# One transformer layer on one core: the routed experts on rows sorted by expert group, in place of every expert on every row

## The chip, the cores and the metric

One core of one Trainium2 chip runs the whole kernel. The metric is the device time in microseconds (us) of one execution, as the median of the runs shown. All arithmetic is in 32-bit floats.

## The reference

The input x has 2048 rows of 256. Layer norm gives xn. Two branches work on xn and are added to x:

- Attention with fast weights. q, k, v and small gates are projected from xn. In chunks of 128 rows, a recurrence takes each chunk's gradients of three fast weight matrices for each of 4 heads, adds momentum, runs five Newton-Schulz iterations on them, adds the result to the weights and scales these to their old row norms. The next chunk needs the new weights, so the 16 chunks are strictly in turn. Beside it stands a windowed softmax attention over 128 + 128 rows. The sum is multiplied by Wo.
- A mixture of experts, cut to what matters:

```
scores = sigmoid(x @ gate_w.T);  sb = scores + gate_bias      # 32 experts in 4 groups of 8
group_scores = sum of the two best sb of each group;  keep the 2 best groups
topi = the 8 best sb of the kept groups
cw = scores at topi / their sum * 2.5, else 0
x_lat = x @ fc1_w.T                                            # 256 -> 128
h = relu(x_lat @ w1[e])**2 * cw[:, e]                          # 128 -> 128, for each expert e
routed = (sum over e of h @ w2[e]) @ fc2_w.T                   # 128 -> 128 -> 256
shared = relu(x @ shared_up.T)**2 @ shared_down.T              # 256 -> 512 -> 256
```

A row has a weight other than 0 for 8 experts at most, and all of these lie in 2 of the 4 groups.

## The kernel before, in words

The kernel is written by hand for five instruction streams (SP for DMA, GpSimd as POOL, ScalarE as ACT, TensorE as PE, VectorE as DVE). Each is executed in its own order and waits on semaphores, named e_... . The order in each stream is the schedule. It is one function, `build` (L74), with an inner function for each piece of work.

There are 16 tiles of 128 rows. Step i (`body(i, last)` in each stream) does the recurrence of tile i and prepares tile m = i + 1. A step has these parts:

- k_side (PE L673, ACT L471, DVE L1067, POOL k_u L331): the products with the fast weights and the gradients' factors, then grads (PE L682), momentum (DVE L1100), the sums for the norm (PE L693, POOL ss_pow L335) and x_first (DVE L1118), which writes X.
- A loop over 20 stages, `for st in range(4 * NI)`, for the two head pairs g = 0 and 1. Four stages are one Newton-Schulz iteration: PE turns X (L697), ACT copies XT (L476), PE makes the Gram product (L703), DVE copies it to Am (L1129), PE squares it (L718), DVE makes Mp (L1134), PE multiplies (L718), DVE makes the new X (L1142). POOL makes aX = a * X at the iteration's start (ax, L339), which DVE's new X needs. After stage st each stream does what its table `fill` has for st: the projections, norms, attention and small gates of tile m or i. This is how all other work is spread through the loop.
- After the loop: update (DVE L1158), row_pow (POOL L345), renorm (DVE L1166, scaling in L1175), turn_w (PE L726) and w_T (ACT L480), which give the next step its weights.

The experts are 8 units (NU) of 4 experts (EU) for each tile. Every expert is computed for every row:

- h_up (PE L825): 4 products of the expert weights with xlT (fc1's result, L805) into the PSUM bank HB.
- h_relu (ACT L507), then h_sq (POOL L358): hr, then hq, 128x512 each.
- y_down (PE L833): 4 products of hq with the second weights into the bank YB.
- y_first (ACT L513) and y_acc (DVE L1321): acc += cw[e] * y, one instruction for each expert (L1328). y_sum (L1331) adds the four parts; turn_y (PE L840), y_T (ACT L537) and out_fc2 (PE L862) end the routed branch in the same bank as the output.

Units 0 and 1 of the next tile are done between the steps, the others at listed places of the step. The routing of tile m is 13 small DVE instructions (route, L1256, rows 128x32 and less), one of which is taken at each half stage after stage 10, and weights (L1316). Layer norm of tile m is ln_stats (L990), prep_rstd on POOL (L287), ln_norm (L998), a transpose on PE (L632) and a copy on ACT (L428). Matmuls issued through a helper are all recorded at L629, ACT's instructions at L426, POOL's powers at L285: go by tile names.

All weights are loaded once at the start (SP L243 to L250, ACT L416 to L423), the two expert tensors with 2 MB each. In a step SP (L261 to L268) loads the next x tile, stores the output tile and loads x again for the residual.

Of the kernel before, what the change touches and what calls it, by code (L numbers as in the profile page):

```python
# [29 lines left out]
F32 = mybir.dt.float32  # L30
AX_X = mybir.AxisListType.X

P = 128
# [13 lines left out]
NU = E // EU  # L47
# [25 lines left out]

def build(nc, x, wall_d, rows_d, wo, fast_d, affine_d, fc1T, fc2T, e1T, e2T, upT, downT, ident_d, fixed_d, out):  # L74
    T = x.shape[0]
    NT = T // P
    LAST = NT - 1
    with ExitStack() as ctx:
        def sb(name, shape):
            return ctx.enter_context(nc.sbuf_tensor(name, shape, F32))  # L80

# [9 lines left out]
        fc1_s = sb("fc1_s", [P, KT, P])  # L91
# [3 lines left out]
        e1_s = sb("e1_s", [P, E, P])  # L95
        e2_s = sb("e2_s", [P, E, P])
# [32 lines left out]
        xa = sb("xa", [P, D])  # L129
        xr = sb("xr", [P, D])  # L130
        ot = sb("ot", [P, D])
        st6 = sb("st6", [P, 6])
        mv = sb("mv", [P, 2])
        rstd = sb("rstd", [P, 2])
        xn = sb("xn", [P, D])
        xnT = sb("xnT", [P, KT, P])
# [6 lines left out]
        z = sb("z", [P, SMALL])  # L143
        sgs = sb("sgs", [P, SMALL - MOM])
# [29 lines left out]
        sbias = sb("sbias", [P, E])  # L174
        g8 = sb("g8", [P, NG, 8])
        gs = sb("gs", [P, 12])
        t8 = sb("t8", [P, 8])
        gm = sb("gm", [P, 12])
        pen = sb("pen", [P, NG])
        msk = sb("msk", [P, E])  # L180
        m8 = sb("m8", [P, 8])
        mr = sb("mr", [P, E])
        csel = sb("csel", [P, E])
        cs1 = sb("cs1", [P, 2])
        cw = sb("cw", [P, E])
        xlT = sb("xlT", [P, P])
        ur = sb("ur", [P, SC, P])
        us = sb("us", [P, SC, P])
        hr = [sb(f"hr{b}", [P, EU, P]) for b in range(2)]
        hq = [sb(f"hq{b}", [P, EU, P]) for b in range(2)]  # L190
        acc = sb("acc", [P, EU, P])
        ya = sb("ya", [P, 2, P])
        ys = sb("ys", [P, P])
        yT = sb("yT", [P, P])
# [11 lines left out]
        def per_group(name):  # L206
# [3 lines left out]
        e_const, e_later, e_up_w, e_down_w, e_ttw, e_init = (sem(n) for n in (  # L210
            "first_const_in", "later_const_in", "up_weights_in", "down_weights_in", "fast_weights_in", "init"))
        e_xa, e_xr, e_stored = sem("xa_in"), sem("xr_in"), sem("stored")
        e_stats, e_aggr, e_veps, e_rstd, e_xn = (sem(n) for n in ("stats", "aggr", "veps", "rstd", "xn_ready"))
# [10 lines left out]
        e_up, e_rn, e_rp, e_wn, e_bd, e_wt, e_WT = (per_group(n) for n in ("upd", "rn", "rp", "Wn", "W1BD", "wt", "WT"))  # L224
# [5 lines left out]
        e_rt, e_cw = sem("route_steps"), sem("cw_ready")  # L230
        e_lr_steps, e_nmx = sem("lr_sum_steps"), sem("max_ready")
        e_fx, e_xlT, e_upm, e_ur, e_us = (sem(n) for n in ("fc1", "xlT", "shared_up", "shared_relu", "shared_sq"))
        e_h, e_hr, e_hq, e_y, e_acc = (sem(n) for n in ("h", "h_relu", "h_sq", "y", "acc"))
        e_ya, e_ys, e_yt, e_yT, e_out, e_ot = (sem(n) for n in ("ya", "y_sum", "y_turned", "yT", "out_mm", "out_ready"))

        NCONST, NLATER, NUP, NDOWN = 2, 3, 3, 3
# [4 lines left out]
        @block.sync  # L241
        def _(sp):
            sp.dma_start(xa[:, :], x[0:P, :]).then_inc(e_xa, 16)  # L243
            sp.dma_start(ident[:, :], ident_d[:, :]).then_inc(e_ident, 16)
            for dst, src in ((wall[:, :, :], wall_d[:, :, :]),
                             (rows[:, :], rows_d.partition_broadcast(P))):
                sp.dma_start(dst, src).then_inc(e_const, 16)
            for dst, src in ((fixed[:, :, :], fixed_d[:, :, :]), (affine[:, :, :], affine_d[:, :, :]),
                             (wo_s[:, :, :], wo.rearrange("(k p) n -> p k n", p=P))):
                sp.dma_start(dst, src).then_inc(e_later, 16)  # L250

            sp.wait_ge(e_xn, 1)
            sp.dma_start(xa[:, :], x[P:2 * P, :]).then_inc(e_xa, 16)
            sp.dma_start(xr[:, :], x[0:P, :]).then_inc(e_xr, 16)

            def store(i, rows):

                sp.wait_ge(e_ot, i + 1)
                sp.dma_start(out[bass.ds(rows, P), :], ot[:, :]).then_inc(e_stored, 16)

            for i in range(NT - 2):  # L261
                here, after, later = i * P, (i + 1) * P, (i + 2) * P

                sp.wait_ge(e_xn, i + 2)
                sp.dma_start(xa[:, :], x[bass.ds(later, P), :]).then_inc(e_xa, 16)
                store(i, here)

                sp.dma_start(xr[:, :], x[bass.ds(after, P), :]).then_inc(e_xr, 16)  # L268
            store(NT - 2, (NT - 2) * P)
            sp.dma_start(xr[:, :], x[LAST * P:T, :]).then_inc(e_xr, 16)  # L270
            store(LAST, LAST * P)
            sp.wait_ge(e_stored, 16 * NT)


        @block.gpsimd
        def _(pool):

            win_scores = Expect(pool, e_as, "win_scores", first=2)
# [86 lines left out]
            def body(i, last):  # L365
                if last:
# [5 lines left out]
                    for u in range(4, NU):  # L372
                        h_sq(i, u)
# [1080 lines left out]
```

## Time and profile before

| what | value |
|---|---|
| median of 3 runs | 831.35 us (829.08 to 831.86) |
| the profiled execution's own time | 830.14 us |
| its span, first to last instruction | 828.1 us |
| PE busy | 780.7 us, 94% |
| DVE busy | 714.6 us, 86% |
| ACT busy | 354.0 us, 43% |
| POOL busy | 406.8 us, 49% |
| bytes moved by DMA | 15.09 MB, of it over 300 GB/s only in the first fortieth |

Busy times are of one execution. The span is what the rows below are measured in; the execution's time is 2.0 us longer. A matmul of 32-bit floats is recorded as two instructions, so x8 is four products, and x24 is twelve small ones.

### The profile page before, as it was taken

What the parts mean: (1) busy time and instruction counts of PE and PEld (TensorE: products, weight loads), DVE (VectorE), ACT (ScalarE), POOL (GpSimd) and SP (SyncE); (2) the same over time, 40 slices, a digit from 0 to 9 for tenths busy, and PEclk for the clock granted to TensorE, in tenths of its full rate; (3) what the DMA queues carried; (4) which work ended last, traced back from release to release, by engine and by line L of the source; (5) the groups of instructions that cost most, each with busy time, mean ns of one, the idle gap of its engine ahead of it and who ended that gap; (6) DMA issues with size and microseconds to landing.
All of it is one profiled execution on the core that took longest, in us unless ns stands there. A gap on an engine that the chain in (4) does not pass through costs nothing.

```text
span 828.1 us, 24889 instructions
## 1 busy us (share of the span) xinstructions
PE 780.7 (94%) x9776; PEld 668.5 (81%) x9776; DVE 714.6 (86%) x2592; ACT 354.0 (43%) x868; POOL 406.8 (49%) x535
## 2 busy tenths in 40 slices
PE   3899999999999999999999999999999999999997
PEld 1888888888888888878888788887888888888886
DVE  4789898898988979889798897988979889898876
ACT  2544344443444434444344444444444444434533
POOL 1654555445454454544555445544465444655442
PEclk9899999999999999999999999999999999999999
DMA  8100000000000000000000000000000000000000
GB/s 321 54 3 14 9 2 21 3 13 9 2 21 2 14 8 2 21 2 15 8 3 20 2 15 9 3 21 2 15 8 2 21 2 15 8 2 15 2 15 7
DMA packets 9811, 15.09 MB, mean 18 GB/s; under 512 B 1120, under 2 KB 8928, under 8 KB 9440
## 3 DMA queue, kind: packets, MB, share of 16 engines
q1 hardware_dynamic: 7904, 7.80, 3.2%
q10 hardware_dynamic: 1792, 5.70, 1.8%
q8 instruction: 78, 1.28, 0.6%
q14 instruction: 37, 0.30, 0.1%
HBM read 11.41 MB, written 2.10 MB: 16 GB/s over the span
## 4 chain that ended last, share of the span: by engine, by line
PE 53%; DVE 33%; issue 6%; ACT 5%; POOL 2%; DMA 1%; SPq 0%; DVEq 0%
PE CC L629 18%; PE M L629 13%; PE HB L629 8%; DVE acc L1328 8%; PE YB L629 8%; DVE Wn L1175 4%; DVE Mp L1138 2%; DVE dhb L1094 2%; DVE X L1146 2%; PE CC L699 2%; DVE Am L1131 2%; POOL r L285 2%; DVE sm L1233 1%; DMA rows<-in_rows 1%; PE CC L700 1%
## 5 line engine op out<-in xcount | busy, mean ns | idle before, releaser
L363 POOL TENSOR_TENSOR hq<-hr 128x512 f32<-128x512 f32 x128 | 137.1, 1071 | 71.9 <-ACT hr L426 71.9
L285 POOL TENSOR_TENSOR r<-r,half 128x3 f32<-128x3 f32 (+1 forms) x78 | 77.9, 1011 | 155.1 <-DVE r L1116 67.9
L629 PE MATMUL HB<-xlT,e_s 128*128 128x128 f32 x1024 | 143.0, 283 | 0.4 <-ACT xlT L426 0.4
L629 PE MATMUL YB<-e_s,hq 128*128 128x128 f32 x1024 | 141.3, 281 | 1.8 <-DVE acc L1328 0.8
L629 PEld LDWEIGHTS HB<-xlT,e_s 128*128 128x128 f32 x1024 | 126.7, 193 | 6.8 <-ACT xlT L426 0.7
L1328 DVE SCALAR_TENSOR_TENSOR acc<-YB,cw,acc 128x128 f32<-128x128 f32 x448 | 125.4, 342 | 7.9 <-PE YB L629 7.9
L341 POOL TENSOR_TENSOR aX<-X,a_tile 128x192 f32<-128x192 f32 x150 | 92.9, 640 | 79.9 <-DVE X L1146 79.9
L426 ACT ACTIVATE hr<-HB 128x512 f32<-128x512 f32 x128 | 76.1, 594 | 128.5 <-PE HB L629 128.5
L629 PEld LDWEIGHTS YB<-e_s,hq 128*128 128x128 f32 x1024 | 124.2, 191 | 7.4 <-issue 4.1
L629 PEld LDWEIGHTS CC<-X,Mp 64*64 64x64 f32 x1800 | 58.3, 135 | 23.6 <-issue 11.3
L629 PEld LDWEIGHTS CC<-Am 64*64 64x64 f32 x1800 | 59.5, 134 | 21.8 <-DVE Am L1131 18.2
L426 ACT ACTIVATE XT<-CC 128x256 f32<-128x256 f32 x150 | 50.8, 381 | 59.7 <-PE CC L700 59.5
L629 PE MATMUL CC<-X,Mp 64*64 64x64 f32 x1800 | 68.6, 222 | 7.6 <-DVE Mp L1138 7.6
L629 PE MATMUL CC<-Am 64*64 64x64 f32 x1800 | 69.8, 223 | 1.9
L1146 DVE SCALAR_TENSOR_TENSOR X<-CC,aX 128x192 f32<-128x192 f32 x150 | 51.3, 352 | 13.4 <-PE CC L629 13.3
L629 PE MATMUL M<-wall,xnT 128*128 128x512 f32 (+1 forms) x128 | 56.9, 551 | 3.6 <-DMA rows<-in_rows 3.6
L629 PEld LDWEIGHTS CC<-XT 64*64 64x64 f32 x1800 | 43.2, 133 | 20.7 <-ACT XT L426 14.7
L1131 DVE COPY Am<-CC 128x192 f32<-128x192 f32 x150 | 48.4, 347 | 9.3 <-PE CC L629 8.3
L1138 DVE SCALAR_TENSOR_TENSOR Mp<-Am,CC 128x192 f32<-128x192 f32 x150 | 49.8, 351 | 7.2 <-PE CC L629 3.6
L629 PE MATMUL CC<-XT 64*64 64x64 f32 x1800 | 55.6, 232 | 0.0
L699 PE MATMUL CC<-ident,X 128*64 128x128 f32 x150 | 39.7, 281 | 0.0
L333 POOL TENSOR_TENSOR kt<-ks 128x128 f32<-128x128 f32 x30 | 13.7, 459 | 51.0 <-ACT ks L426 51.0
(180 smaller groups left out, 1525.3 us busy)
## 6 DMA issues: line engine op xcount, KB each, us to landing
xa<-in_x SPq DMA_DIRECT2D x16, 128.0 KB, 2.1
e_s<-in_e1T ACTq DMA_DIRECT2D x1, 2048.0 KB, 12.7
e_s<-in_e2T ACTq DMA_DIRECT2D x1, 2048.0 KB, 19.3
xr<-in_x SPq DMA_DIRECT2D x16, 128.0 KB, 2.2
out<-ot SPq DMA_DIRECT2D x16, 128.0 KB, 1.7
wall<-in_wall SPq DMA_DIRECT2D x1, 820.0 KB, 7.1
up_s<-in_upT ACTq DMA_DIRECT2D x1, 512.0 KB, 15.9
down_s<-in_downT ACTq DMA_DIRECT2D x1, 512.0 KB, 20.0
```

What stands on the lines that cost most here:

```text
L285: return pool.tensor_tensor(dst, src, expo[:, 0:n], ALU.pow)
L341: pool.tensor_tensor(aX[g][:, :, :].rearrange("p w c -> p (w c)"), X[g][:, :, :].rearrange("p w c -> p (w c)"), a_tile[:, it, :], ALU.mult ...
L363: pool.tensor_tensor(hq[b][:, :, :], hr[b][:, :, :], hr[b][:, :, :], ALU.mult).then_inc(e_hq, 1)
L426: return nc.scalar.activation(out_, in_, func, **kw)
L629: return pe.matmul(out_, lhsT, rhs, start=start, stop=stop)
L699: pe.transpose(CA[g][0:HD, 0:P], X[g][:, 0, :], ident[:, :])
L1094: tt(dhb[g][:, :], kt[g][:, 0, :], dhi[g], ALU.mult)
L1131: nc.vector.tensor_copy(Am[g][:, :, :], CC[g][:, 0:6 * P].rearrange("p (w c) -> p w c", w=3)[:, :, 0:HD])\
L1138: nc.vector.scalar_tensor_tensor(Mp[g][:, :, :].rearrange("p w c -> p (w c)"), Am[g][:, :, :].rearrange("p w c -> p (w c)"), b / c, CA[g][ ...
L1146: nc.vector.scalar_tensor_tensor(X[g][:, :, :].rearrange("p w c -> p (w c)"), CB[g][:, 0:3 * HD], NS[it][2], aX[g][:, :, :].rearrange("p w ...
L1175: ins = nc.vector.tensor_scalar(Wn[g][:, w, :], Wn[g][:, w, :], r3[g][:, 5, w:w + 1], nrm[g][:, w:w + 1], ALU.mult, ALU.mult)
L1328: ins = nc.vector.scalar_tensor_tensor(acc[:, e, :], y, w, acc[:, e, :], ALU.mult, ALU.add)
```

## The change

The routing of all 16 tiles is done once, early, and the rows are copied, sorted by group, to a DRAM tensor. A row goes there twice, once for each of its two groups. Each group begins a new tile of 128 sorted rows; 2 x 16 + 3 = 35 tiles (NJ) hold every case. A sorted tile belongs to one group and needs 8 experts, 2 units. Rows that fill up a tile are zero. Part by part:

- x is loaded whole at the start in three DMAs. Layer norm of all tiles is done in step 0 (tile 0 and the first four ahead of it): statistics on DVE, the normalising itself on ACT, transposes into HB in pairs. fc1 and the gate projection are one matmul of 160 columns (gate_rows), for pairs of tiles, in step 0 and at the start of step 1. ACT writes fc1's result twice to xsrc, as row-major rows.
- DVE's route() is 46 steps on all tiles at once, two a stage from step 1, stage 1. They include the group of each row by comparisons, prefix sums over rows (one product on PE, prefixes) and over tiles (four doublings), the group that owns each sorted tile (owner_i), the places of each row (dest_i) and the 8 weights of each copy, which stand behind the row's 128 numbers (ROW = 136).
- POOL issues 32 indirect DMAs (scatter), two a stage from step 2, stage 6, after the work listed for the stage. From step 13, stage 17, it issues 32 more (gather), one a stage, and the rest in the last step.
- Expert units: seven up and seven down slots a step, n = 7 i + k - 24, the down unit two slots later. The first up unit is slot 3 of step 3, the last down unit slot 4 of step 13. Steps 0, 1, 2 and 14 have none. ACT does relu and square in place (h_relu); DVE multiplies with the gate weights before the down product (h_weight, 128x512), so all 8 experts add up in PSUM. y_acc, y_first, y_sum and POOL's h_sq go.
- SP loads for each sorted tile the 8 experts of its group (two DMAs of 512 KB, at an address from a register), the rows, writes their 8 weights to DRAM and reads them back spread over all partitions (512 KB), and stores the tile's result. Three buffers (RING) turn. It also writes 2.4 MB of zeros to the sorted tensor at the start.
- total writes x + attention + shared to x_all. After the last step eight rounds for two tiles each add the two gathered rows (last_sum), transpose, copy, multiply by fc2 (last_turn, last_yT, last_fc2), add (last_out) and store.

The diff, cut to its core:

```diff
@@ sync
+            def load(j):
+                b = j % RING
+                if j >= RING:
+                    sp.wait_ge(e_y, HALVES * (j - RING + 1))
...
+                first = sp.value_load(owner_i[0:1, j:j + 1], min_val=0, max_val=E - EPG)
+                sp.dma_start(e1_s[b][:, :, :], e1T[:, bass.ds(first, EPG), :]).then_inc(e_tile[b], 16)
+                sp.dma_start(e2_s[b][:, :, :], e2T[:, bass.ds(first, EPG), :]).then_inc(e_tile[b], 16)
+            def gather_rows(j):
+                if j == 0:
+                    sp.wait_ge(e_scat, 16 * 2 * NT)
+                sp.dma_start(xs[b][:, :], xs_d[j * P:(j + 1) * P, :]).then_inc(e_rows[b], 16)
+            def spread(j):
+                sp.wait_ge(e_rows[b], 16 * (n + 1))
+                sp.dma_start(cw_d[j, :].rearrange("(p e) -> p e", p=P), xs[b][:, P:ROW]).then_inc(e_gate[b], 16)
+                sp.wait_ge(e_gate[b], 32 * n + 16)
+                sp.dma_start(cwb[b][:, :], cw_d[j, :].partition_broadcast(P)).then_inc(e_gate[b], 16)
+            for j in range(RING, NJ):
+                keep(j - RING)
+                load(j)
+                gather_rows(j)
+                spread(j)
@@ gpsimd
+            def scatter(n):
+                t, j = n // 2, n % 2
+                if n == 0:
+                    pool.wait_ge(e_rt, RT_ALL)
...
+                pool.indirect_dma_start(
+                    xs_d[:, :], bass.IndirectOffsetOnAxis(ap=dest_i[:, t, j:j + 1], axis=0),
+                    xsrc[:, t, j, :], None).then_inc(e_scat, 16)
-            def h_sq(i, u):
...
+                    if (SCAT_STEP, 6) <= (i, st) and moved:
+                        if i > 5:
+                            if (i, st) >= GATHER_AT:
+                                moved.pop(0)()
+                        elif len(moved) > 2 * NT:
+                            moved.pop(0)()
+                            moved.pop(0)()
                 for g in range(G):
                     row_pow(m, g)
@@ scalar
+            def h_relu(i, k):
...
+                a(flat, HB[:, :], ACT.Relu).then_inc(e_hs, 1)
+                act.wait_ge(e_hs, 2 * n + 1)
+                a(flat, flat, ACT.Square).then_inc(e_hs, 1)
@@ tensor
-                fill = {2: [lambda: q_out(i), lambda: prep_turn(m)], 3: [lambda: y_down(i, 2)],
...
+                fill = {2: [lambda: q_out(i)], 3: [lambda: h_slot(i, 2)],
                         4: [lambda: prep_qk(m)], 5: [lambda: prep_qk_more(m)], 6: [lambda: prep_v(m)],
+                        7: [lambda: y_slot(i, 3)], 8: [lambda: prep_mom(m)],
+                        9: [lambda: prep_turn_v(m), lambda: h_slot(i, 3)], 10: [lambda: y_slot(i, 4)],
                         11: [lambda: att_scores(i, False)], 12: [lambda: prep_turn_qk(m)],
+                        13: [lambda: h_slot(i, 4)],
+                        15: [lambda: att_turn_p(i, False), lambda: y_slot(i, 5)], 16: [lambda: att_pv(i)],
+                        17: [lambda: h_slot(i, 5)], 18: [lambda: turn_comb(i)],
+                        19: [lambda: out_down(i, 0), lambda: out_down(i, 1)]}
@@ vector
+            def h_weight(i, k):
...
+                gate = cwb[b][:, :].rearrange("p (t e) -> p e t", e=EPG)[:, c:c + EU, :]
+                nc.vector.tensor_tensor(hb[n % RING][:, :, :], hb[n % RING][:, :, :], gate, ALU.mult).then_inc(e_hw, 1)
+                fill = {0: [lambda: h_weight(i, 0), lambda: att_scale(i)], 2: [lambda: h_weight(i, 1)],
...
-                        if st > 10 and routing:
+                        if routing and (i, st) >= (SORT_STEP, 1):
                             routing.pop(0)()
```

## Rows read from the trace of the kernel before

**Rows 1.** The page of the profile: busy times, and the chain that ended last

```profile
PE 780.7 (94%) x9776; PEld 668.5 (81%) x9776; DVE 714.6 (86%) x2592; ACT 354.0 (43%) x868; POOL 406.8 (49%) x535
...
PE 53%; DVE 33%; issue 6%; ACT 5%; POOL 2%; DMA 1%; SPq 0%; DVEq 0%
PE CC L629 18%; PE M L629 13%; PE HB L629 8%; DVE acc L1328 8%; PE YB L629 8%; DVE Wn L1175 4%; DVE Mp L1138 2%; DVE dhb L1094 2%; DVE X L1146 2%; PE CC L699 2%; DVE Am L1131 2%; POOL r L285 2%; DVE sm L1233 1%; DMA rows<-in_rows 1%; PE CC L700 1%
```

**Rows 2.** Critical chain, whole span (start us, us, what): the scaling of the weights

```profile
75.78 1.48 DVE Wn L1175 x3
...
794.99 1.49 DVE Wn L1175 x3
```

**Rows 3.** Stretches: length, busy PE, PEld, DVE, ACT, POOL, clock; last acc's DVE, ACT

```profile
294.80:330.00 35.20, 34.49 (x516) 29.07 (x515) 31.48 (x114) 15.51 (x37) 19.53 (x26) 1.00 0.02 6
...
286.10:337.45 51.35, 49.60 (x639) 42.56 (x638) 45.60 (x167) 22.26 (x55) 25.92 (x35) 1.00 0.03 10
...
294.80:330.00 35.20, 7.83 (x28) 0.00 (x0) 1.00 0.02 6
```

**Rows 4.** Critical chain in one step, the same columns

```profile
295.21 0.89 PE YB L629 x8
...
302.00 0.11 PE CC L699
...
304.97 0.84 PE CC L629 x24
305.81 1.23 PE M L629 x4
```

**Rows 5.** Timeline of DVE, then POOL (start, us, engine, line, what)

```profile
287.59 1.12 DVE L1094 TENSOR_TENSOR dhb<-kt,ks 128x128 f32<-128x128 f32 x1
...
289.44 0.28 DVE L1094 TENSOR_TENSOR dhb<-kt,ks 128x128 f32<-128x128 f32 x1
...
295.48 1.13 DVE L1001 TENSOR_SCALAR xn<-xa,mv,rstd 128x256 f32<-128x256 f32 x1
...
287.48 1.08 POOL L363 TENSOR_TENSOR hq<-hr 128x512 f32<-128x512 f32 x1
```

**Rows 6.** The page, a costliest group (busy, mean ns, idle before)

```profile
L363 POOL TENSOR_TENSOR hq<-hr 128x512 f32<-128x512 f32 x128 | 137.1, 1071 | 71.9 <-ACT hr L426 71.9
```

**Rows 7.** Groups by shape: ACT's relu and copy, DVE's; last a timeline row

```profile
L426 ACT ACTIVATE hr<-HB 128x512 f32<-128x512 f32 x128 | 76.1, 594 | 128.5 <-PE HB L629 128.5
...
L426 ACT ACTIVATE XT<-CC 128x256 f32<-128x256 f32 x150 | 50.8, 381 | 59.7 <-PE CC L700 59.5
...
L1131 DVE COPY Am<-CC 128x192 f32<-128x192 f32 x150 | 48.4, 347 | 9.3 <-PE CC L629 8.3
...
L1030 DVE TENSOR_TENSOR qkn<-sl,r 128x512 f32<-128x512 f32 x16 | 11.1, 692 | 0.6
...
L992 DVE BATCH_NORM_STATS2 st<-xa 128x6 f32<-128x256 f32 x16 | 6.7, 421 | 0.0
...
315.87 0.36 DVE L1268 MAX8 g<-sbias 128x8 f32<-128x8 f32 x4
```

**Rows 8.** Critical chain at the start

```profile
12.09 5.10 PE M L629 x8
```

**Rows 9.** SP's issue, the landing of a load (page), POOL's ax and a power

```profile
799.49 0.34 SPq L259 DMA_DIRECT2D out<-ot  x1
...
xa<-in_x SPq DMA_DIRECT2D x16, 128.0 KB, 2.1
...
302.90 1.14 POOL L341 TENSOR_TENSOR aX<-X,a_tile 128x192 f32<-128x192 f32 x2
...
L285 POOL TENSOR_TENSOR r<-r,half 128x8 f32<-128x8 f32 x16 | 26.2, 1636 | 41.1 <-DVE r L1020 41.1
```

**Rows 10.** Timeline of PE and DVE in the last step

```profile
812.87 0.66 PE L787 MATMUL M<-ident,pr 128*128 128x128 f32 x4 [1.05 <-ACT pr L426]
...
825.53 0.42 DVE L1341 TENSOR_TENSOR ot<-M,xr 128x256 f32<-128x256 f32 x1 [1.49 <-PE M L629]
```

More of the change, by code:

```diff
@@ new lines, in y_unit, with turn_tile, ln_turn @@
+        def y_unit(i, k):
+            n = PER * i + k - FIRST - 2
+            return n if 0 <= n < UNITS else None
+        def turn_tile(i, k):
+            n = PER * i + k - FIRST - 2
+            j = 0 if n == -2 else (n + 3) // 2 if n >= -1 and n % 2 else NJ
+            return j if j < NJ else None
+        def ln_turn(i, k, half):
+            order = {(0, 0): 1, (0, 1): 2, (1, 1): 3, (2, 1): 4, (3, 1): 5, (4, 1): 6, (5, 1): 7, (6, 1): 8}
+            return order.get((k, half)) if i == 0 else None
@@ L250, in _ @@
                 sp.dma_start(dst, src).then_inc(e_later, 16)
[L252 to L268, printed above, removed]
@@ new lines, in keep @@
+            def keep(j):
+                sp.wait_ge(e_yo, j + 1)
+                sp.dma_start(y_d[j * P:(j + 1) * P, :], yo[j % 2][:, :]).then_inc(e_ysto[j % 2], 16)
+            for j in range(RING):
+                load(j)
+            for j in range(RING):
+                gather_rows(j)
+                spread(j)
+            for j in range(RING, NJ):
+                keep(j - RING)
+                load(j)
+                gather_rows(j)
+                spread(j)
+            for j in range(NJ - RING, NJ):
+                keep(j)
@@ L403, in _ @@
             prep_n8(0)
-            window(0, True)
+            for n in range(1, 5):
+                prep_rstd(n)
+            window(0)
             prep_kl(0)
-            h_sq(0, 0)
             body(0, False)
@@ new lines, in y_slot @@
+            def y_slot(i, k):
+                n = y_unit(i, k)
+                if n is not None:
+                    j, b = n // HALVES, n // HALVES % RING
+                    pe.wait_ge(e_hw, n + 1)
+                    if n % HALVES == 0:
+                        pe.wait_ge(e_yo, j)
+                        pe.wait_ge(e_xsT, min(j + 2, NJ))
+                    for e in range(EU):
+                        first, final = n % HALVES == 0 and e == 0, n % HALVES == HALVES - 1 and e == EU - 1
+                        ins = mm(YB[:, 0:P], hb[n % RING][:, e, :], e2_s[b][:, n % HALVES * EU + e, :], first, final)
+                    ins.then_inc(e_y, 1)
+                j = turn_tile(i, k)
+                if j is not None:
+                    turn_rows(j)
+                extra(i, k, 0)
@@ new lines, in extra, with last_turn @@
+            def extra(i, k, half):
+                n = ln_turn(i, k, half)
+                if n is not None:
+                    ln_turned(n)
+                n = gate_pair(i, k, half)
+                if n is not None:
+                    gate_rows(n)
+            def last_turn(n):
+                pe.wait_ge(e_ys, n + 1)
+                pe.wait_ge(e_yT, n)
+                for l in range(2):
+                    ins = pe.transpose(HB[:, l * P:(l + 1) * P], ys[:, l, :], ident[:, :])
+                ins.then_inc(e_yt, 1)
@@ new lines, in best_marked, with run, chosen, chosen_sum @@
+                def best_marked(part):
+                    def run():
+                        for t in range(part * 4, part * 4 + 4):
+                            ins = nc.vector.match_replace(mr[:, t, :], m8[:, t, :], msk[:, t, :], TAKEN)
+                        return ins
+                    return run
+                def chosen():
+                    return stt(csel[:, :, :], mr[:, :, :], TAKEN, sc[:, :, :], ALU.is_equal, ALU.mult)
+                def chosen_sum():
+                    return nc.vector.tensor_reduce(csum[:, 0, :], csel[:, :, :], AX_X, ALU.add)
```

824 lines of the change are left out of this document (506 added, 318 removed).

## The prediction, made before the change was run

> **What bounds the kernel now.** The page comes first: PE is busy 94% of the span and DVE 86%, with the clock granted in full over a whole step [rows 1, 3]. Two engines that full need the chain. It goes through PE for 53% and through DVE for 33%, and the expert work is on it three times: the up products (HB) with 8%, the down products (YB) with 8% and the weighted sum (acc) with 8% [rows 1]. The critical chain in order of time gives the rhythm: the scaling of the fast weights (L1175) stands there once a step, at 75.78 for step 0 and at 794.99 for step 14 [rows 2], so a step lasts 719.21 / 14 = 51.37 us. The span is 75.8 to the end of step 0, then 14 steps, then 33.1 us.
>
> A step has two halves. In the Newton-Schulz part (294.8 to 330.0) PE is busy 34.5 of 35.2 us and DVE 31.5; the other 16.15 us are mostly a serial chain [rows 3]. On the chain PE's pure times can be read: one expert unit (four experts) is 0.89 us, two transposes are 0.22, a group of products for both halves is 0.84, 616 columns of projection 1.23 [rows 4].
>
> A third thing is hidden in DVE's rows: the copy called dhb lasts 1.12 us for group 0 and 0.28 us for group 1, and the long one begins 0.11 us after POOL's 1.08 us squaring hq and ends 0.15 us after it [rows 5]. DVE with two SBUF inputs stands behind POOL.
>
> **The change, part by part.** Durations are of the profiled execution: span 828.1, its own time 830.14 (2.0 outside the span), 1.2 under the median 831.35.
>
> *Expert units.* Now 16 x 8 = 128 up and 128 down units. Afterwards 35 tiles x 2 = 70 and 70. 116 x 0.89 = 103 us of PE leave, also all 128 hq of POOL, 137.1 us [rows 6], and the acc of DVE, 7.8 us in each Newton-Schulz part alone [rows 3]. What this is worth depends on where units stay: they run from the middle of step 3 to the middle of step 13, seven up and seven down a step; steps 0, 1, 2 and 14 have none.
>
> *A step without experts.* Outside Newton-Schulz only the 0.85 us of the held dhb go: 15.3. In it, PE without its 11 units is 35.2 - 9.8 = 25.4; DVE without acc (7.8 [rows 3]), routing (about 3.0, thirteen small instructions) and the normalising xn (1.1) is 31.5 - 11.9 = 19.6; the pure alternation of one group (two transposes, ACT's 0.38, three products, three DVE instructions of 0.35 [rows 4, 7]) is some 3.5 x 5 = 17.5. PE is last, and since it must now wait for the alternation at times I take 27. Bare step: 42.3.
>
> *A step with seven and seven.* Newton-Schulz loses two units (1.8), two transposes (0.2), fc1 (0.45) and gains row transposes (0.3): 33.0, less 0.3 for DVE's waits that go, since DVE falls to 19.6 + 6 x 0.69 = 23.7 (h_weight priced by qkn, 128x512 with two SBUF inputs, 692 ns [rows 7]). 15.3 + 32.7 = 48.0. ACT squares in place of POOL: 7 x 0.6 us more [rows 7], covered, since ACT is busy 43% [rows 1].
>
> *Start.* The 4 MB of expert weights no longer load beside wall and rows, on which PE waits until 12.09 [rows 8]; that can give 2.4 us. The tiles 1 to 4 of layer norm stand in DVE's queue ahead of step 0 (7 x 0.6 plus small), and a unit that held up the transposes of qkn goes. I take 1.8 us earlier.
>
> *Step 0.* Bare, plus 8 pairs of tiles transposed (8 x 0.44) and 6 gate pairs (640 columns, 1.28 each by the 1.23 for 616 [rows 4]): 11.2 us of PE, and 8 tiles of statistics on DVE (0.42 + 0.18 + 0.15 each [rows 7], 6.0). About half lies in gaps: +5.5. So the first 75.8 become 75.8 - 1.8 - 9.05 + 5.5 = 70.5.
>
> *Step 1: the sort.* Routing of all 16 tiles at two instructions a stage. Maxima and matches do not shrink with batching: 64 maxima at 0.09 (four take 0.36), 16 at 0.12, 16 matches at 0.19; then three 128x512 at 0.69 and some 27 small ones at 0.2 [rows 7]: 19 us. DVE in Newton-Schulz: 19.6 + 19 = 38.6, and at the 0.9 it reaches today, 42.7. Step: 58.
>
> *Step 2: the scatters.* 8 routing steps are left (five 128x512 among them, 4.6 us): +3.5. Then 32 indirect DMAs leave POOL two a stage. **No row shows one.** The nearest from below is SP's plain DMA issue, 0.34 us; from above the 2.1 us from an issue to its landing; between them lie POOL's own instructions, 0.57 for half a pair of ax, 1.08 for hq, 1.64 for a power of 128x8 [rows 5, 9]. An indirect one must read 128 indices and make a row transfer from each, POOL's kind of work: I take c = 1.1, nearest to POOL's rows, and keep 0.34 and 2.1. The Trainium skill, page "DMA: Bandwidth & Descriptors", section "Latency and other measured facts", puts the first byte of a GpSimd DMA at about 1 us, emission included; by c = 1.0 the sum would be 4 us less. No run here shows it yet.
> Behind the scatters stand ax, prep_n8, window, prep_kl and the row_pow that the renormalisation waits for. From the ax of stage 8: 24c plus three pairs of ax (1.15), n8 1.64, window and kl some 3.3 (six small copies and products), that is 8.4 + 24c. Row_pow is wanted three iterations (27 / 5 = 5.4 each) and 2.1 us later, 18.3. Excess 24c - 9.9 = 16.5 (0 at the lower end, 40.5 at the upper). Step 2: 62.3.
>
> *Step 3.* SP can fetch rows only when all scatters have landed, PE wants them in stage 7: 46 for four up and two down units, 1.5 for rows a little late. 47.5. *Steps 4 to 12:* 9 x 48.0 = 432. *Step 13,* three up and five down: 46. *Step 14* is bare, with 20 gathers, one a stage: POOL's load is five pairs of ax 5.75, two instructions of 1.02, n8 1.64, window and kl 3.3, that is 12.7 + 20c, against 27 + 2.1 = 29.1; excess 5.6 at 1.1: 47.9.
> *SP's queue,* per tile: store, register load, two 512 KB loads, rows, spread, broadcast. With 2.1 us a landing [rows 9], three landings in series and about 5 us for bulk it is some 13 us from the last down unit of the tile three back; the weighting comes three slots, 18 us and more, later. Nothing.
>
> *Last step.* Without its 14 units its own chain surfaces and total starts near 814.6 in place of 825.53 [rows 10]. Then eight rounds that now exist: sum, transposes, ACT copy, fc2, final add. The first takes 3.1, the rest are bound by YB being single: the add (0.69) and two fc2 products (1.0) with two hops, 1.87 each: 13.1. 831.2 + 2.1 store, 5.2 more than now: 38.3.
>
> **Sum.** 70.5 + 58 + 62.3 + 47.5 + 432 + 46 + 47.9 + 38.3 = 802.5; + 2.0 = 804.5 against 830.14; + 1.2 for the median: 806.
>
> **Rivals.**
> - *POOL becomes the bound, and the kernel is slower.* Place: POOL's queue in step 2 (stages 8 to 19) and step 14. Price 44 us for each us of c, break-even c = 1.67; at 2.1 it is 850. For: POOL's pow on 8 columns takes 1.64 us, so software per column is dear. Against: most POOL rows are near 1. 0.14.
> - *Tiles come late over SP.* If the 13 us are 20, half of the 35 tiles cost 2 us each: 841. For: the broadcast is 512 KB after two dependent landings. Against: the slack above. 0.06.
> - *The alternation is the bound in bare steps.* If Newton-Schulz bare is 31 and not 27, five steps give 20 back: 826. For: where PE has less to do, in the last step, it already waits 1.05 us at a time [rows 10]. Against: two groups alternate. 0.13.
> - *DVE and POOL hold each other up.* h_weight has two SBUF inputs and stands right where POOL runs ax; at 0.8 us once a step, ten steps cost 8: 814. Against: xn stands there today and is held just so, 1.13 us for half the columns [rows 5]. 0.10. The Trainium skill, page "SBUF — State Buffer", section "Who interferes with whom", says that such a DVE instruction and a GpSimd one that reads SBUF exclude each other. By that rule, the trace agrees (1.12 against 0.28).
> - *More than forecast.* c near 0.6 (22 less, of which step 2 gives 12) and full steps at 47: 780. For: DVE leaves the bound altogether. 0.15.
> - *It does less than it says.* "Sorted" halves nothing: 35 of 64 possible group tiles are always worked, the worst case whatever the data. That is in the sum.
> Forecast: 0.42.
>
> **How the numbers follow.** 806 is the likeliest case. Its own range is 795 to 820 (0.9 us on each of nine full steps, c from 0.9 to 1.35). For 8 in 10 the range goes down to the better case and up into POOL's and SP's: 783 to 843. About 0.3% (2.5 us) is what a measurement can tell from no change. Slower takes POOL's and SP's cases, 0.19; same takes the edge of the alternation's, 0.04; faster the rest, 0.77.
>
> **What would show it.** Right: L1175 returns every 48 us between steps 4 and 12; near 42 plus POOL's excess in 14; dhb at 0.28 in both groups; one step of 60 or more in the third place, its ns_x waiting for aX; a POOL row for the scatters near 1.1 us. Wrong: a full step that stays at 50 or over (then something else than the count of units carries it); DVE waiting for gate rows; PE waiting for rows or weights in steps 4 to 13; a granted clock that falls in the bare steps or the rounds, which rows of today, full almost everywhere, don't foretell.

## The result: 873 us, not 806

The changed kernel takes 872.92 us, median of 4 runs (871.12 to 873.96); the kernel before took 830.81 beside it (829.08 to 831.86). The ratio is 1.0507, 95% interval 1.0479 to 1.0534: 42 us slower, where 25 us faster was forecast, and 30 us past the upper end of the range. The profiled execution took 871.12 us with a span of 869.1, so 2.0 us lie outside the span, as in the sum.

The page of the changed kernel, busy time and chain, answers to [rows 1]:

```profile
PE 725.5 (83%) x8887; PEld 601.1 (69%) x8887; DVE 612.8 (71%) x2050; ACT 366.9 (42%) x895; POOL 359.6 (41%) x465
...
PE 58%; DVE 17%; POOL 9%; ACT 8%; issue 6%; DMA 1%; SPq 0%; POOLq 0%; DVEq 0%; ACTq 0%
```

The work has left as counted: PE is busy 83% in place of 94%, DVE 71% in place of 86%. An engine that is busy less while the kernel takes longer stands waiting somewhere. To find where, the span is cut at the first scaling of the fast weights in each step (L1385, L1175 in the kernel before). The windows of the changed kernel, one line for steps 2, 3, 7, 8, 14 and the last (columns: window, its us, busy us and instruction count of PE, PEld, DVE, ACT and POOL, granted clock, DMA share, GB/s):

```profile
125.80:194.70 68.90, 43.03 (x500) 33.51 (x500) 36.45 (x122) 15.96 (x40) 44.11 (x54) 0.77 0.12 41
194.70:245.80 51.10, 43.49 (x551) 35.11 (x551) 36.51 (x117) 21.33 (x52) 23.27 (x30) 0.91 0.17 52
...
404.20:456.60 52.40, 47.90 (x616) 40.85 (x616) 39.28 (x119) 25.60 (x62) 19.75 (x25) 0.96 0.36 110
456.60:510.00 53.40, 48.63 (x615) 41.73 (x615) 39.80 (x119) 24.94 (x60) 19.67 (x25) 0.94 0.38 120
...
769.90:821.90 52.00, 37.85 (x500) 28.99 (x500) 33.65 (x113) 15.85 (x40) 36.80 (x46) 0.93 0.10 27
821.90:869.10 47.20, 30.66 (x116) 23.03 (x116) 18.04 (x48) 9.37 (x23) 11.24 (x12) 0.75 0.17 57
```

Measured against the forecast, in us: start and step 0 72.4 (70.5), step 1 53.4 (58), step 2 68.9 (62.3), step 3 51.1 (47.5), steps 4 to 12 together 475.8 (432), step 13 48.2 (46), step 14 52.0 (47.9), last 47.2 (38.3). The nine full steps are 44 of the 67 us by which the sum fell short, and each of them, at 52.4 to 53.4, is longer than the 51.4 of the kernel before, with half the expert work in it.

**The end of a full step** shows why. The chain of waits of the changed kernel, in order of time, at the end of step 8 (start, us, what):

```profile
502.74 1.92 PE M L790 x8
504.66 0.89 PE YB L790 x8
505.56 0.87 PE M L790 x4
506.42 0.91 PE HB L790 x8
...
507.35 0.61 ACT hb L546
...
507.98 0.64 ACT hb L546
...
508.64 1.08 DVE hb L1643
...
510.04 0.76 DVE Wn L1385 x3
```

And its timeline (start, us, engine, line, operation; in brackets the idle time before it and what ended it):

```profile
508.64 1.08 DVE L1643 TENSOR_TENSOR hb<-hb,cwb 128x512 f32<-128x512 f32 x1 [3.22 <-ACT hb L546]
...
510.86 0.85 PE L920 MATMUL CC<-ident,Wn 128*64 128x128 f32 x3 [3.55 <-DVE Wn L1385]
```

The weighting h_weight(i, 6) stands in DVE's queue between the update and the renormalisation. It needs the up unit of slot 6, which is the last thing in PE's queue before the transposes of the new weights. So PE works through output products, down unit and up unit, ACT does two passes, DVE multiplies, and only then may DVE scale the weights for which PE stands. Two engines wait for each other in turn: DVE 3.22 us, then PE 3.55 us. In the kernel before, y_sum stood at this place of DVE's queue (331.68 us in one step), but its inputs were there and it waited for nothing; the up units that PE did just before its transposes belonged to the next tile, and nothing ahead of the scaling needed them.

PE's wait has an echo. Windows of 2.5 us after the same point one step earlier (columns as above):

```profile
456.60:459.10 2.50, 1.43 (x6) 0.73 (x7) 2.35 (x12) 0.65 (x2) 0.00 (x0) 0.50 0.70 265
459.10:461.60 2.50, 2.50 (x9) 2.14 (x8) 0.74 (x3) 1.20 (x4) 0.19 (x1) 0.50 0.03 2
461.60:464.10 2.50, 2.50 (x18) 2.50 (x18) 2.03 (x10) 0.94 (x3) 0.72 (x2) 0.70 0.68 210
464.10:466.60 2.50, 2.50 (x38) 2.31 (x37) 2.45 (x9) 0.00 (x0) 0.00 (x0) 1.00 0.00 0
```

The granted clock is at half, 1.2 GHz, in the first two windows, in which PE is busy for 1.43 and for all of the 2.50 us, and it is back at full in the fourth. The Trainium skill, page "TensorE: Matmul & The Clock Gate", section "What's actually happening", says that a gate sets the clock by how busy the engine has been of late; by that rule, the trace agrees, with 0.50 after the wait.

**Step 2.** POOL's timeline in the changed kernel:

```profile
150.06 1.22 POOL L410 DMA_INDIRECT sorted_rows<-xsrc,dest_i  x1 [0.18 <-issue]
151.59 0.97 POOL L410 DMA_INDIRECT sorted_rows<-xsrc,dest_i  x1 [0.30 <-issue]
152.86 0.97 POOL L410 DMA_INDIRECT sorted_rows<-xsrc,dest_i  x1 [0.30 <-issue]
154.14 0.96 POOL L410 DMA_INDIRECT sorted_rows<-xsrc,dest_i  x1 [0.30 <-issue]
155.13 1.14 POOL L465 TENSOR_TENSOR aX<-X,a_tile 128x192 f32<-128x192 f32 x2
```

A scatter holds POOL for 0.97 us and 0.30 us pass before the next: c is 1.27, where 1.1 was taken. The chain of step 2 runs through these rows.

### The profile page after: what moved, and what is told of

It is laid out like the page before. It is cut to its first block, busy times and chain, and to the rows that moved or that the text cites. A ratio compares the mean times of both kernels' runs of the same rounds, so it can differ in the third digit from the quotient of the medians.

```text
span 869.1 us, 22591 instructions
## 1 busy us (share of the span) xinstructions
PE 725.5 (83%) x8887; PEld 601.1 (69%) x8887; DVE 612.8 (71%) x2050; ACT 366.9 (42%) x895; POOL 359.6 (41%) x465
## 4 chain that ended last, share of the span: by engine, by line
PE 58%; DVE 17%; POOL 9%; ACT 8%; issue 6%; DMA 1%; SPq 0%; POOLq 0%; DVEq 0%; ACTq 0%
PE CC L790 21%; PE M L790 15%; PE YB L790 8%; PE HB L790 7%; POOL sorted_rows L410 3%; ACT hb L546 3%; DVE Wn L1385 3%; POOL r L395 2%; POOL xsrc L420 2%; PE CC L920 1%; DVE hb L1643 1%; ACT L730 1%; POOL aX L465 1%; ACT XT L546 1%; DVE Am L1341 1%
## 5 line engine op out<-in xcount | busy, mean ns | idle before, releaser
L465 POOL TENSOR_TENSOR aX<-X,a_tile 128x192 f32<-128x192 f32 x150 | 117.2, 799 | 133.3 <-DVE X L1356 127.8
L1643 DVE TENSOR_TENSOR hb<-hb,cwb 128x512 f32<-128x512 f32 x70 | 81.9, 1170 | 33.8 <-ACT hb L546 33.0
L1341 DVE COPY Am<-CC 128x192 f32<-128x192 f32 x150 | 48.2, 353 | 52.2 <-PE CC L790 50.8
L920 PE MATMUL CC<-ident,Wn 128*64 128x128 f32 x96 | 23.7, 378 | 67.7 <-DVE Wn L1385 67.7
L546 ACT ACTIVATE hb<-HB 128x512 f32<-128x512 f32 x70 | 41.5, 593 | 90.0 <-PE HB L790 90.0
L790 PE MATMUL HB<-xsT,e_s 128*128 128x128 f32 x560 | 78.0, 282 | 0.0
L790 PE MATMUL YB<-e_s,hb 128*128 128x128 f32 x560 | 77.0, 280 | 0.0
L790 PE MATMUL CC<-X,Mp 64*64 64x64 f32 x1800 | 73.1, 231 | 3.0 <-DVE Mp L1348 1.8
L790 PEld LDWEIGHTS HB<-xsT,e_s 128*128 128x128 f32 x560 | 68.7, 191 | 3.2
L546 ACT ACTIVATE XT<-CC 128x256 f32<-128x256 f32 x150 | 51.3, 382 | 46.2 <-PE CC L884 46.0
L790 PEld LDWEIGHTS YB<-e_s,hb 128*128 128x128 f32 x560 | 68.7, 191 | 2.9
L920 PEld LDWEIGHTS CC<-ident,Wn 128*64 128x64 f32 x96 | 10.8, 141 | 78.2 <-DVE Wn L1385 77.3
L1348 DVE SCALAR_TENSOR_TENSOR Mp<-Am,CC 128x192 f32<-128x192 f32 x150 | 51.8, 352 | 14.8 <-PE CC L790 13.3
L546 ACT ACTIVATE WT<-CC 64x192 f32<-64x192 f32 x64 | 20.7, 323 | 80.4 <-PE CC L920 80.0
## 6 DMA issues: line engine op xcount, KB each, us to landing
x_all<-in_x SPq DMA_DIRECT2D x1, 1408.0 KB, 15.3
```

Of the source, the lines that this page charges most:

```text
L465: pool.tensor_tensor(aX[g][:, :, :].rearrange("p w c -> p (w c)"), X[g][:, :, :].rearrange("p w c -> p (w c)"), a_tile[:, it, :], ALU.mult ...
L546: return nc.scalar.activation(out_, in_, func, **kw)
L790: return pe.matmul(out_, lhsT, rhs, start=start, stop=stop)
L920: ins = pe.transpose(CA[g][0:HD, w * P:(w + 1) * P], Wn[g][:, w, :], ident[:, :])
L1341: nc.vector.tensor_copy(Am[g][:, :, :], CC[g][:, 0:6 * P].rearrange("p (w c) -> p w c", w=3)[:, :, 0:HD])\
L1348: nc.vector.scalar_tensor_tensor(Mp[g][:, :, :].rearrange("p w c -> p (w c)"), Am[g][:, :, :].rearrange("p w c -> p (w c)"), b / c, CA[g][ ...
```

## Experiments

They were made in four sittings, each of kernels measured together on one chip: e1 to e4, e5 to e7, e8 to e10 (on the chip of e5 to e7), e11 to e14. The kernel before took 829.5 to 830.7 us in all four. Why it matters which kernels share one comes at e8. e2, e3 and e4 ran once each, so of these only the steps are used.

**e1: the weighting behind the renormalisation.**

```
                 update(i)
-                h_weight(i, 6)
                 renorm(m)
                 w_bd(m)
                 total(i)
+                h_weight(i, 6)
```

> The seventh h_weight of a step moves from between update and renorm to behind total on DVE; nothing else changes. Theory W (DVE, held by that instruction, delays the scaling of the weights, and PE, which then stands idle, runs the next products at the lower clock): the 3.2 us wait and the 1.1 us of the instruction leave the chain in steps 3 to 12, so ten steps lose about 3.4 us each, and about 1 us more from the clock; full steps go from 52.7 to 48.5, the whole from 872.9 to about 830. Rival S (the strided gate operand, 1.08 us instead of 0.69, carries the full steps): the move changes the step by under 1 us, the whole stays above 862.

844.99 us (840.99 to 848.0, 4 runs), ratio 1.0186, interval 1.0157 to 1.0215. Steps 7 and 8 in the windows of e1:

```profile
394.80:443.00 48.20, 46.52 (x617) 39.81 (x616) 39.17 (x119) 25.52 (x62) 19.72 (x26) 1.00 0.38 120
443.00:491.60 48.60, 46.56 (x618) 40.17 (x618) 39.50 (x119) 24.86 (x60) 19.63 (x26) 1.00 0.42 132
```

One line moved by four brings a full step from 52.9 to 48.5 us on average, within 0.5 of the forecast's 48.0, with the clock full and PE busy 46.6 of 48.6. The whole was expected at about 830 and missed that by 15: step 14 is 59.0 here where the changed kernel's first profile had 52.0, and step 2 is 71.8 for 68.9; e8 comes back to this. PE's first transposes now wait 0.23 us for the scaling:

```profile
492.46 0.25 PEld L920 LDWEIGHTS CC<-ident,Wn 128*64 128x64 f32 x3 [0.23 <-DVE Wn L1385]
```

**e2: the gate operand read in line.** The weighting lasts 1.08 us even alone, against 0.69 for qkn of the same size; its gate operand is read at a stride of eight elements. Here it is contiguous (the weights then go to other tokens).

```
-gate = cwb[b][:, :].rearrange("p (t e) -> p e t", e=EPG)[:, c:c + EU, :]
+gate = cwb[b][:, :].rearrange("p (e t) -> p e t", e=EPG)[:, c:c + EU, :]
```

> h_weight reads the gate weights from consecutive places (they are then the wrong weights; only the time is of interest), at its old place. Rival S: each of the 70 falls from 1.08 to about 0.69 us and all of it is on the path, the whole falls by 25 us. Theory W: the duration falls the same, but only the one between update and renorm is on the chain: 10 x 0.4 = 4 us, the whole is 867 to 870.

887.46 us. The same row in the groups of instructions, the changed kernel and then this one:

```profile
L1643 DVE TENSOR_TENSOR hb<-hb,cwb 128x512 f32<-128x512 f32 x70 | 81.9, 1170 | 33.8 <-ACT hb L546 33.0
```

```profile
L1643 DVE TENSOR_TENSOR hb<-hb,cwb 128x512 f32<-128x512 f32 x70 | 54.2, 774 | 37.5 <-ACT hb L546 36.7
```

28 us of DVE go, and a full step stays at 52.0 to 53.5. The whole misses what either side expected, by steps in which nothing was changed: step 14 is 61.3, step 2 71.9. The size of the instruction was mis-priced in the forecast (0.69 for 1.17), but it isn't what a step lasts for; its place is.

**e3: four scatters in place of 32** (28 of them are left out, so most rows that the experts read are zeros; SP waits for four).

```
+if n >= 4:
+    return
```

> 28 of the 32 scatters are left out (most sorted rows stay zero), the rest as changed. Theory P (POOL's queue is the bound of step 2 from stage 8 on): step 2 falls from 68.9 to 44 to 48 us, its clock from 0.77 back to 0.9 or more, the whole by 22 to 25 us, to about 849. Rival (step 2 is long because of the routing on DVE and because PE has little to do): it falls by under 8 us.

859.34 us. Steps 2 and 3:

```profile
130.20:176.50 46.30, 35.24 (x500) 26.39 (x500) 36.23 (x122) 15.88 (x40) 20.83 (x30) 1.00 0.19 63
176.50:225.10 48.60, 40.18 (x551) 32.59 (x551) 36.23 (x117) 21.36 (x52) 19.26 (x26) 1.00 0.05 11
```

With 4 scatters in place of 28, step 2 is 46.3 us, where the forecast without any had 45.8. The 24 that are gone are the 22.6 us to the 68.9 of the changed kernel's first profile, and the 25.5 to 25.7 us to the 71.8 and 72.0 of e1 and e4 in the same sitting. PE busy falls from 43.0 to 35.2 for the same 500 instructions: at a granted 0.77 they had lasted longer. The whole was expected at about 849 and missed by 10, as step 14, with its gathers unchanged, is 60.6, and step 1 57.3 for 53.4.

**e4: PE kept busy before the transposes,** in steps 3 to 12, with products that nobody reads.

```
+if h_unit(i, 6) is not None:
+    for _ in range(4):
+        mm(M1[:, :], ident[:, :], wall[:, 0, 0:2 * D])
```

> In steps 3 to 12 PE does four products of 128x512 on data nobody reads (3.4 us) while it would stand before turn_w, waiting for the scaled weights; the wait of DVE stays as it is. It tells the wait from the clock behind it. Theory W: the granted clock of those steps returns to 1.00, the products behind the wait (k_side, q_side) take 2 us less, in all a full step loses 1 to 2 us: 855 to 863. Rival (the clock costs nothing there, since DVE and ACT are last): unchanged within 2 us, or 5 us longer where the four products end later than the weights come.

880.31 us. A full step is 51.8 with the clock at 1.00:

```profile
463.70:515.50 51.80, 49.90 (x624) 41.51 (x623) 39.68 (x119) 24.96 (x60) 19.68 (x25) 1.00 0.38 124
```

The four products end at 516.24, as the first scaled weights come at 516.30, and DVE's wait is still 3.22 us: they fill PE's wait and hold up nothing. So of the 4.4 us that e1 gives a step, about 1 (52.9 to 51.8) is the half clock and 3.4 the mutual wait. The whole missed its 855 to 863, with 60.6 in step 14 and 72.0 in step 2.

**e5: the clock held in step 2, step 14 and the last step,** on top of e1.

```
+def idle_products(count):
+    for _ in range(count):
+        mm(HB[:, :], ident[:, :], wall[:, 0, 0:2 * D])
```

> The kernel with h_weight(i,6) late, and idle products (128x512 on the identity into HB, read by nobody): one a stage in step 2, one in every second stage of step 14, and 2, 1, 3, 1, 1 between the links of the last step's chain. The late-weight kernel is 845.0 us; its granted clock is 0.74 in step 2, 0.83 in step 14 and 0.76 in the last step. Theory K (the clock falls because PE stands, and a doubled product time then lies on the chain): the clock returns to 0.95 or more in the three stretches; last step 46.8 to 40, step 14 from 59 to 51, step 2 from 71.8 to 67 (POOL's scatters stay its bound), the whole 820 to 828. Rival P (PE's clock is no bound there; POOL, DVE and hops are): the idle products only add their own 0.22 us each, steps 2 and 14 stay within 1 us of 72 and 59, the last step gets 1 to 2 us longer, the whole 845 to 849.

(In steps 2 and 14 PE also waits at the start until HB is free.) 841.05 us (840.92 to 845.81), ratio 1.015. In steps 2 and 14 rival P holds: the clock rises (0.74 to 0.91 and 0.83 to 0.89), the steps last 73.1 and 60.5, a little longer. PE is not what they wait for. In the last step theory K has the direction: 46.8 becomes 43.0, where 40 was expected. An idle product takes 0.86 us and not the 0.22 of the expectation, and they stand on this step's chain with 5.65 us, so 3.8 is what is left after them. The last output products (12 instructions; start, us) on the chain of the changed kernel, and of e5:

```profile
844.06 5.00 PE M L790 x12
```

```profile
816.42 2.59 PE M L790 x12
```

The same products at the two clock levels, 2.4 us apart in one row. The whole was expected at 820 to 828 and missed, since steps 2 and 14, which carried most of it, did not move.

**e6: one scatter a stage,** from stage 4 of step 2; the first unit three slots later, the gathers from stage 0 of step 14; on top of e1.

```
-if (SCAT_STEP, 6) <= (i, st) and moved:
+if (SCAT_STEP, 4) <= (i, st) and moved:
...
-    moved.pop(0)()
```

> The kernel with h_weight(i,6) late, one scatter a stage from stage 4 of step 2 in place of two from stage 6, the first expert unit three slots later, and the gathers from stage 0 of step 14. Theory C (32 scatters at 0.98 plus 0.30 us fill POOL between the ax of the stages, 1.27 each; it is their density that step 2 waits for): half of them go under step 3, where POOL has room; step 2 from 71.8 to 52 to 58, step 3 from 51.0 to 50 to 53, the whole 825 to 833. Rival N (POOL's work is the same in sum and the excess only moves into step 3): step 2 gives 10 and step 3 takes 8 to 10, the whole 842 to 846.

831.37 us (10 runs, 828.94 to 833.94), ratio 1.0009: no difference from the kernel before. Against e1, step 2 falls from 71.8 to 56.3 and step 3 rises from 51.0 to 58.0. About half of the gain moved on, between theory C and rival N.

**e7: both.**

> Both edits at once, the idle products of steps 2, 3 and 14 in every second stage. If theories K and C both hold and their gains are separate: step 2 near 50, step 14 near 51, last step near 40, the whole 800 to 812, below the kernel before (830.7). If the clock in step 2 and 14 only followed POOL's wait (rivals P and N), no more than e6 gives, less the idle products: 825 to 846.

837.48 us, ratio 1.008: 25 above the range for theories K and C, and within the 825 to 846 of rivals P and N. The idle products cost more in step 14 (63.0 for e6's 59.6) than they gave; in the last step the clock fell in the closing rounds instead (2.07 us for a round's two fc2 products in place of 1.12), and 47.3 us were left.

**e8 and e10: the gathers moved.** Of the 20 gathers in step 14, e8 leaves 14 there and e10 none; the rest go into POOL's queue in the last step.

```
-if (i, st) >= GATHER_AT:
+if (i, st) >= GATHER_AT and (st < 8 or st % 2):
```

> The kernel of one scatter a stage (831.4 us) with 14 of the 32 gathers in step 14 in place of 20: one a stage up to stage 7, then one in every second stage; the other 18 go into POOL's queue in the last step. Theory C (each gather holds POOL for 1.27 us, and step 14 waits for POOL): step 14 from 59.6 us to 48 to 51 (6 gathers, 7.6 us, and a backlog that does not build up); in the last step 18 x 1.27 = 23 us of POOL's time go beside 24 us of products, so it stays at 45 to 47; the whole 820 to 824. Rival K (step 14 is long because PE's clock is 0.80 there and the gathers lie beside it): step 14 stays within 2 us of 59.6, the whole 830 to 833.

> The kernel of one scatter a stage with no gather in step 14 and all 32 in the last step. Step 14 is then bare, what the forecast put at 42.3 us. Theory C: 43 to 46 us there with the clock near 1.00 (a step 2 without scatters took 46.3 with some routing in it); the last step waits for gathers, 32 x 1.27 = 41 us from the renormalisation's powers, less the 25 us that its chain takes: 45 + 12 to 16 = 57 to 61, the whole 829 to 834. Rival K: step 14 is 55 or more with the clock below 0.9 even without a gather.

e8 took 816.49 us (813.74 to 818.28, ratio 0.9833, interval 0.9809 to 0.9856), e10 832.58 (ratio 1.0035). e8's last step is 53.7, where 45 to 47 were expected. Step 14 of e8, then of e10:

```profile
717.20:762.70 45.50, 36.71 (x508) 28.61 (x508) 32.08 (x113) 16.14 (x41) 30.95 (x40) 0.96 0.08 23
```

```profile
717.00:762.70 45.70, 38.19 (x508) 29.93 (x508) 31.95 (x113) 16.12 (x41) 17.05 (x26) 0.93 0.01 3
```

14 gathers cost step 14 nothing, and a bare step is 45.7 us, where 42.3 was forecast. But e8 gave more than theory C allows: its step 3 was 50.0 against 58.0 in e6, although up to there the two kernels have the same instructions in the same order on every engine. The groups of waits of e6 name something that e8, e9, e10 and the changed kernel's first profile do not have (engine, line, releaser: us in total, times, longest):

```profile
DVE X L1355 <- remote: 13.5, 6, 2.6
DVE Mp L1347 <- remote: 9.2, 7, 1.8
...
DVE Am L1340 <- remote: 2.7, 2, 1.6
```

(DVE's three of five groups; the other two are ACT's.) "Remote" is a releaser that the trace can't name. The same X in e6's timeline, then in e8's:

```profile
209.23 0.56 PE L789 MATMUL CC<-X,Mp 64*64 64x64 f32 x12 [0.70 <-DVE Mp L1347]
...
211.77 0.62 DVE L1355 SCALAR_TENSOR_TENSOR X<-CC,aX 128x192 f32<-128x192 f32 x2 [2.59 <-remote]
```

```profile
208.29 0.92 PE L789 MATMUL CC<-X,Mp 64*64 64x64 f32 x24
...
208.90 0.71 DVE L1355 SCALAR_TENSOR_TENSOR X<-CC,aX 128x192 f32<-128x192 f32 x2 [0.40 <-PE CC L789]
```

In e6 its products ended by 209.79 and its aX long before, and yet X begins 2.0 us later.

**e9: gathers spread as in e8, idle products in the last step alone.**

> The same with the idle products in the last step alone (2, 1, 3, 1, 1 between the links of its chain; none in steps 2, 3 and 14). Theory: the long products between renormalisation and the last sum take 2.6 us in place of 5.0 and 4.4 in place of 6.4, as they did where the last step's clock was held before; last step 41 to 43, the whole 816 to 820. Rival: the clock falls in the eight closing rounds instead and gives the gain back: last step 45 to 47, the whole as the kernel without idle products.

813.56 us (811.3 to 818.46), ratio 0.9818, interval 0.9775 to 0.986: the lowest time of all, though its runs and e8's overlap. Its last step is 50.6 (53.7 in e8), not 41 to 43: its chain runs through POOL's 18 gathers, the last of which begins at 794.76 and takes 2.5 us to land; the fifth of the eight sums, which needs the last 16 gathers, starts then, at 797.27. e10, with 32 there, has a last step of 69.6, where 57 to 61 were expected: the rounds can't begin before the gathers of their half have landed. That its whole still fell into the expected 829 to 834 is luck: its steps 2 and 3 are 12 us shorter than e6's, with the same instructions.

**e11 to e14: four kernels again, in one sitting.** e11 is the changed kernel, e12 is e1, e13 is e6, e14 is e9, unchanged.

> The changed kernel as it is, again, beside the three below in one sitting. In the sittings of the first seven experiments DVE stood up to 2.6 us at a time before X and Mp in the steps with indirect DMAs, with a releaser that the trace can't name; in the first profile of the changed kernel and in the last sitting it never did. Theory U (those waits belong to the sitting, not to the kernel): all four kernels of this sitting show them, or none does; if none, this one is 868 to 874 us with step 14 near 52. Rival B (they belong to the build, how its instructions lie): this one has none, 871 to 874, the next two have them.

> h_weight(i,6) late, again. Theory U with none in this sitting: step 14 from 59.0 to 52, the whole 845.0 to 836 to 840, full steps 48.4 as before. Rival B: 841 to 848 again, step 14 59.

> One scatter a stage, 20 gathers in step 14, again. Theory U with none in this sitting: step 3 from 58.0 to 50 (as the two kernels of the last sitting, whose steps 2 and 3 have the same instructions), step 14 from 59.6 to 50 to 53, the whole 831.4 to 816 to 822; then the 14.9 us that spreading the gathers seemed to give were mostly the sitting's, and 6 gathers are worth 5 to 8. Rival B: 829 to 834 again.

> Gathers spread and the last step's clock held, again: 811 to 818 if the waits are absent, 825 to 832 if they are there (steps 2, 3 and 14 longer by 8 each at most).

| kernel | first | again | step 2 | step 3 | step 14 | last |
|---|---|---|---|---|---|---|
| the changed one | 872.92 | 887.05 | 68.9, 71.7 | 51.1, 54.8 | 52.0, 59.1 | 47.2, 45.1 |
| e1, e12 | 844.99 | 841.37 | 71.8, 71.9 | 51.0, 51.0 | 59.0, 58.8 | 46.8, 46.7 |
| e6, e13 | 831.37 | 834.78 | 56.3, 56.2 | 58.0, 59.2 | 59.6, 60.2 | 45.1, 45.8 |
| e9, e14 | 813.56 | 838.45 | 53.3, 56.6 | 50.0, 58.7 | 44.7, 54.5 | 50.6, 56.1 |

Theory U holds: all four kernels of this sitting have the unnamed waits, the identical e9 and e14 differ by 25 us, and rival B falls with them. The kernel before, without indirect DMAs, took 830.5 here too. In e11 those of DVE stand in steps 2, 3 and 14 and nowhere else; in e3, with 4 scatters but all gathers, in step 14 alone. ACT has them too, and longer. In step 2 of e11:

```profile
174.44 1.11 PE L970 MATMUL M<-ident,pr 128*128 128x128 f32 x4
...
182.60 0.36 DVE L1356 SCALAR_TENSOR_TENSOR X<-CC,aX 128x192 f32<-128x192 f32 x1 [5.38 <-remote]
...
182.66 0.60 ACT L546 ACTIVATE prT<-M 128x512 f32<-128x512 f32 x1 [8.78 <-remote]
```

ACT waits there only for these four transposes, whose record ends 7.1 us earlier (0.03 us earlier in the changed kernel's first profile), and DVE, which waits for other products of PE, is let go 0.06 us before it. e12 has the same two waits, 5.38 and 8.78 us. So a cause in DVE alone, such as its port, doesn't explain them. They come only in steps where indirect DMAs are issued, only in some sittings, and the sittings with and without them include the same chip (e5 to e7 with, e8 to e10 without).

Pairs inside this sitting give the prices. Weight moved: 887.05 to 841.37, 45.7 us, of which 4.4 in each full step. Scatters thinned: 841.37 to 834.78, 6.6 us (15.7 less in step 2, 8.2 more in step 3). Six gathers and the idle products of the last step: step 14 gets 5.7 shorter (60.2 to 54.5), the last step 10.3 longer, the whole 3.7 slower.

## Why the prediction was wrong, by its steps

- **The 15.3 us outside Newton-Schulz in "15.3 + 32.7 = 48.0", carried over to the step with seven and seven units, is the step that failed.** It priced seven weightings (6 x 0.69 in Newton-Schulz and the rest hidden) by DVE's total load and never asked what stands behind the seventh in the queue and what it waits for. 4.4 us a full step (e11 against e12), so 40 of the 67 missing us, and most of the 3.8 by which e12's step 3 is the shorter. It should have been read from the diff: last unit of PE's queue, two ACT passes, then DVE, then the scaling, then PE. With the row moved, 48.0 was right to 0.5 us, and so were the counts behind it. None of the rivals was this one; the nearest, DVE and POOL holding each other up, speaks of the same instruction and of another cause. That hold exists, POOL's aX lasts 799 ns on average for 640 before and 716 in e2, but full steps of 48.5 in e1 leave it no part in the loss.
- **"I take c = 1.1" was 1.27.** The formula 24c - 9.9 then gives 20.6 in place of 16.5 and a step of 66.4; 68.9 was measured, and 22.6 over the 46.3 of e3. The rival that POOL bounds the kernel names the right place, but c stayed below its break-even of 1.67; alone it would not have made the kernel slower. No row showed a scatter when c was chosen; the c = 1.0 that the prediction also names would have been further off.
- **Step 14.** The bare step was put at 42.3 and is 45.7 (e10): 3.4 of the 4 us that the alternation's rival gave a step, and PE, busy 38.2 of 45.7, isn't the bound there. Formula and bare step erred in opposite ways: 20 gathers add 6.3 to it (52.0 in the changed kernel's first profile, both without unnamed waits), 5.6 was forecast.
- **Step 1**, 58 forecast, 53.4: DVE is busy 46.2 us, 12.6 more than in the bare step 14 (33.65), where the routing was put at 19. It hid 4.6 us of the error elsewhere. In the other runs step 1, unchanged, is 53.4 to 57.3, at a granted clock of 0.90 down to 0.81 and without any unnamed wait or indirect DMA; why is open.
- **"831.2 + 2.1 store", the last step, 38.3 for 47.2.** Rounds were put at 1.87 and are 1.97, 0.8 us in all. The rest is the chain ahead of them at half clock: total at 849.08, 27.2 us after the scaling, where 19.6 was taken. The M row alone doubles, 2.59 to 5.00.
- **The clock.** The prediction lists a fall of it among what would make it wrong, and put no number on it. It costs about 1 us in a full step (e4). In the last step idle products give 3.8 between two sittings (e1 to e5) and 3.1 within one (e8 to e9). In steps 2 and 14 they raised the clock and shortened nothing (e5).
- **Slips of the sum.** The parts listed for the sort add up to 18.2 us, not 19, and the better case's "22 less" counts step 14 below its floor: 12 + 5.6 + 9 give its 780. Neither changes the outcome.
- **Right:** dhb is short in both groups, 0.29 us on average; SP's tiles are late once, by 0.4 us; the work counts hold. Of the waits of PE for rows or weights in steps 4 to 13, which were to be a sign of being wrong, this is the only one.

## What to carry to other kernels

When an instruction is put into an in-order queue, write down the latest thing it waits for and everything behind it in the same queue before pricing its duration; one instruction of 1.08 us cost 4.4 us here because two engines then waited for each other in turn. A kernel freed of work gains only if the chain that remains is shorter too, and here a PE left to stand for 3.55 us also gave up its clock. When identical kernels differ between sittings, take prices only from pairs in one sitting.

## What had not been expected of the hardware

- A granted clock of 0.50 through 5 us after a wait of some 3.6 us, PE being busy 3.9 of them; four idle products that fill the wait bring full steps from 0.94 to 0.97 to 1.00.
- An indirect DMA of 128 rows occupies POOL for 0.94 to 1.22 us with 0.30 to the next, scatter and gather alike (means 984 and 988 ns).
- A multiplication of 128x512 on DVE whose second operand is read at a stride of eight elements took 1.08 us and up, 774 ns on average with that operand in line.
- Waits of DVE of up to 5.4 us and of ACT of up to 8.8 us with no releaser that the trace names, in two looked at closely 2.0 and 7.1 us after all that they need had ended, in steps with indirect DMAs, in three sittings of four (the first profile of the changed kernel, taken before these, had none either). Between identical kernels such a step differs by 3 to 10 us. What makes them is open: that DVE and ACT are let go together fits a late signal from PE, but no kernel here separates that from other causes. So it is also open whether a sorted version beats the kernel before: e9 did by 1.8% in one sitting, and the same kernel was 1.0% slower in another.
